# First round's indices loaded as four columns by two small transfers, its rows gathered by them, and the first query product ahead of the counts

## The chip, the cores and the metric

The kernel runs on one core of one Trainium2 chip. The metric is the device time of one execution in microseconds. Before the change three runs gave 676.91, 676.98 and 677.72, so the median is 676.98 us. The profiled execution took 677.21 us.

## What is computed

10,000 nodes with 512 features each (`x`) and 5,000 edges, sorted by destination (`src`, `dst`). One attention layer over the graph, then a small feed-forward layer and three normalisations:

```python
q = (h @ Wq).reshape(n, H, DK)          # H = 8 heads
k = (h @ Wk).reshape(n, H, DK)
v = (h @ Wv).reshape(n, H, DK)
e = jnp.einsum('ehd,ehd->eh', k[src], q[dst]) / sqrt(DK)
m = segment_max(e, dst);  ex = exp(e - m[dst]);  z = segment_sum(ex, dst)
a = segment_sum((ex / z[dst])[:, :, None] * v[src], dst)
x1 = layernorm(h + a @ Wo)
f = relu(x1 @ W1 + b1) @ W2 + b2
out = layernorm(h + layernorm(x1 + f))
```

Products are done once per edge, on gathered rows `x[dst]` and `x[src]`, and not once per node.

## The kernel before, in words

The 5,000 edges are worked through in 10 rounds of 500. A round gathers the 500 destination rows and 500 source rows (four indirect transfers of 125 rows each, `GXD` and `GXS`), turns them on TensorE (`TXD0` to `TXD3`, `TXS0` to `TXS3`, line 1025), splits each turned block into a high part (ScalarE, L521) and a low part (VectorE, L761), and multiplies: `Q0` to `Q3`, `K0` to `K3`, `V0` to `V3`, `O0` to `O3`. Each of these steps is 12 matmuls at L965: four blocks k of the contraction by three combinations (high by high, high by low, low by high). The scores, a running softmax in order of the edges and the feed-forward part for 1,000 rows of output per round (the slots `N0`, `N1`, `E0`, `E1`) follow.

Each engine has its order of steps written out: `PLAN` gives every step a due time, and `sequence` sorts by it. Steps with `!` are done once, ahead of or in round 0. In every engine the queue is strictly in that order; engines wait on each other by semaphores.

What happens once, at the start:

- SyncE loads the indices as 40 rows of 125 (`dst`, `src`, and `dst` shifted by one, L341 to L346), then Wq, Wk, small columns, W1 and the row of destinations (L348 to L357). It waits for the destination rows of round 0 (`xd_loaded`) before it issues Wv and W2 (L359, L361), and for the source rows (`xs_loaded`) before the rest, Wo last (L364 to L368).
- GpSimd sets constants (L378 to L409; among them `iota_b`, L398, 128 by 1024). Then come the gathers of round 0 (L412), which wait for the tables `dst_idx` and `src_idx`.
- VectorE casts the raw indices to floats (`CAST`, L657 and L660), TensorE turns them (`TURN`, L974 and L977), and VectorE writes the tables (`TABS`, L677 to L684). So an index passes a transfer, a cast, a transpose and a cast before a row is gathered by it.
- The rest of VectorE's chain (`FLAG`, `FILLI`, `DIG`) and TensorE's `OFFS` and `TURNF` prepare a list of the nodes that are no destination. It is made by counting: `CNT0` to `CNT4` on VectorE build one-hot tiles (L648, L643), two of each in turn, and `COUNT0` to `COUNT4` on TensorE multiply them (8 matmuls each, L1001). `CNT2` can only start when `COUNT0` is done, as it writes over the first buffer.
- `HQ` on ScalarE (L499) and `LQ` on VectorE (L636) split Wq into its high and low part.
- `FILLERS` puts matmuls whose result is not read (L1118) behind some steps: 8 behind `TURNF`, 2 behind each of `COUNT0`, `COUNT1`, `COUNT2`, 4 behind `TXD1`, 3 behind `TXD3`.

Order of the first steps before the change:

```
TensorE: TURN OFFS TURNF COUNT0 COUNT1 TXD0 TXD1 TXD2 TXD3 COUNT2 Q0 Q1 TXS0 TXS1 COUNT3 COUNT4 TXS2 Q2 ...
VectorE: CAST FLAG TABS FILLI DIG CNT0 CNT1 LQ TXD0 TXD1 CNT2 TXD2 TXD3 CNT3 CNT4 TXS0 TXS1 LK ...
ScalarE: HQ TXD0 TXD1 TXD2 TXD3 Q0 HK Q1 TXS0 TXS1 TXS2 HV TXS3 HO Q2 Q3 ...
```

Turned blocks go in turn to two banks (`pT`), so `TXD2` waits until the low part of block 0 has been taken, and `TXD3` for that of block 1. Products go in turn to three banks (`pP`). A product waits before its first matmul for all four low parts of its weights and of its rows.

Of the kernel before, what the change touches and what calls it, by code (L numbers as in the profile page):

```python
# [8 lines left out]
I32 = mybir.dt.int32  # L9
U32 = mybir.dt.uint32  # L10
# [12 lines left out]
SLOT_PERIOD = {"N0": 7687, "N1": 7689}  # L23
PLAN = {
    "pe": """
!TURN -276034; !FOLD -51782; !OFFS -237181; !TURNF -205187; !COUNT0 -202748; !COUNT1 -198663; !COUNT2 -146723;
!COUNT3 -94502; !COUNT4 -90190; !ROFF -71911; !BITS -8816; TXD0 -189819 -22912 125030 125323 125345;
TXS0 -102406 26305 131951 131437 131817; Q0 -138628 34546 131782 132194 129672; K0 -59911 65956 133983 133320 137209;
V0 27356 105501 136738 136738 170605; O0 89451 141151 143013 157654 247834; TXD1 -186065 -14365 126120 126712 125690;
TXS1 -100425 38188 132022 131705 131969; Q1 -106115 57936 132236 132221 132162; K1 -40813 69908 134313 133555 140512;  # L30
V1 33080 113889 136894 136880 181017; O1 106767 141614 143149 165755 248144; TXD2 -166405 -7868 129028 130799 126518;
# [43 lines left out]
E1.sq3 148558 148885 149937 229129 359991; <E1.z 149166 150501 150260 232611 340778  # L75
""",
    "dve": """
!CAST -263381; !FLAG -243336; !TABS -242836; !FILLI -241863; !FW -55094; !B1 -55229; !LQ -172721; !LK -85485;
!LV -54432; !LO 76605; !CNT0 -198287; !CNT1 -179760; !CNT2 -159099; !CNT3 -97504; !CNT4 -91086; !RANK -79616;
!DIG -211902; !LIST -79575; TXD0 -162172 -29587 125840 127315 124482; TXS0 -89151 40059 130890 130776 132032;  # L80
K0 -51732 66249 133633 132533 134452; W0 18249 122663 136307 136222 169476; N0 35421 125323 136834 136488 170118;
G0 49521 129368 137409 137177 185919; L0 44048 128784 137153 137940 187035; H0 89910 140875 142983 151481 211814;
TXD1 -161904 -24476 126177 127482 124895; TXS1 -88968 56437 131385 130810 132286;
K1 -49832 70573 134038 133868 136053; W1 29856 124303 136862 136864 179193; N1 42403 127213 136981 137078 182926;
G1 68839 133170 137965 140178 189672; L1 64124 130892 138184 139311 192048; H1 97516 140880 143008 152925 213212;
TXD2 -144446 7080 128832 130128 126147; TXS2 -67230 58549 131944 130850 132506; K2 -33982 77307 134316 133913 138039;
W2 61679 130905 137933 139380 191352; N2 70023 134152 138251 141899 191579; G2 76092 136480 140628 154187 213723;
L2 72234 139296 139912 145223 200118; H2 101683 143459 143493 165349 227378; TXD3 -114588 26350 129097 130197 126490;
TXS3 -57609 63218 132044 131711 132622; K3 -31718 80817 134898 134139 143486; W3 68959 138928 138383 140291 192894;
N3 81190 139073 139358 144215 193343; G3 111076 141990 141868 162698 225022; L3 84326 139475 140817 145509 203217;  # L90
H3 120939 144076 143627 166956 228551; mask -45989 55213 129213 134970 144639; A1 -39956 75393 134721 134045 136739;
# [69 lines left out]
def graph_attention(nc, x, src, dst, Wq, Wk, Wv, Wo, g1, be1, g2, be2, W1, b1, W2, b2, out):  # L161
    N, D = x.shape
    E = src.shape[0]
    DFF = W1.shape[1]
    P = 128
    KC = D // P
    HD = P // HEADS
    DK = D // HEADS
    R = 125
    EG = KC * R  # L170
# [6 lines left out]
    with ctx:  # L177
        def sb(name, shape, dt=F32):
            return ctx.enter_context(nc.sbuf_tensor(name, shape, dt))
# [23 lines left out]
        edge_idx = sb("edge_idx", [P, CT], I32)  # L203
        node_idx = sb("node_idx", [P, CT], I32)
        is_last = sb("is_last", [R, CT])

        xs = sb("xs", [P, 4, D])
        xd = sb("xd", [P, 4, D])
# [11 lines left out]
        weight = sb("weight", [P, EG])  # L220
# [50 lines left out]
        column_b = hots[:, 2 * (P + NL) * T8:2 * (P + NL) * T8 + NL]  # L271
        row_b, column_no, repeat_total = (att[:, 0, 100 + CT * n:140 + CT * n].bitcast(BF16)[:, 0:CT] for n in range(3))

        names = """dst_loaded idx_loaded wq_loaded wk_loaded wv_loaded wo_loaded w1_loaded b2_loaded w2_loaded all_loaded row_loaded
        zero_set ident_set ident_done head_set head_done below_set below_done iota_done init_done
        idx_cast idx_turned repeat_set repeat_summed offs_ready offs_done offs_kept fill_set fill_turned tables_done fill_kept
        split_hi split_lo w1_done b1_folded b1_done bias_loaded bits_set tables_clear
# [35 lines left out]
        def pP_of(i, step):  # L313
            return pP[place[i, step] % 3]
# [23 lines left out]
        @block.sync  # L338
        def _(sp):
            on = Waits(sp.wait_ge, s)  # L340
            sp.dma_start(idx_raw[0:CT, 1, :], dst.rearrange("(t e) -> t e", e=R)).then_inc(s["dst_loaded"], 16)  # L341
            sp.dma_start(idx_raw[0:CT, 0, :], src.rearrange("(t e) -> t e", e=R)).then_inc(s["idx_loaded"], 16)
            on.wait_ge("zero_set", 1)
            sp.dma_start(idx_raw[0:CT - 1, 2, :], dst[1:1 + (CT - 1) * R].rearrange("(t e) -> t e", e=R))\
                .then_inc(s["idx_loaded"], 16)
            sp.dma_start(idx_raw[CT - 1:CT, 2, 0:R - 1], dst[1 + (CT - 1) * R:E].rearrange("(t e) -> t e", t=1))\  # L346
                .then_inc(s["idx_loaded"], 16)
            sp.dma_start(stage["q"], Wq.rearrange("(k p) n -> p k n", p=P)).then_inc(s["wq_loaded"], 16)  # L348
            sp.dma_start(stage["k"], Wk.rearrange("(k p) n -> p k n", p=P)).then_inc(s["wk_loaded"], 16)
            with nc.allow_non_contiguous_dma("short columns, once"):  # L350
                sp.dma_start(g1_col[:, :], g1.rearrange("(k p) -> p k", p=P)).then_inc(s["w1_loaded"], 16)
                sp.dma_start(be1_col[:, :], be1.rearrange("(k p) -> p k", p=P)).then_inc(s["w1_loaded"], 16)
                for h in range(2):
                    sp.dma_start(b1_col[DFF * h:DFF * h + DFF, :], b1.rearrange("(f a) -> f a", a=1)).then_inc(s["w1_loaded"], 16)
            sp.dma_start(w1_raw, W1.rearrange("(k p) f -> p k f", p=P)).then_inc(s["w1_loaded"], 16)
            on.wait_ge("zero_set", 2)
            sp.dma_start(dst_row[:, 1:EG + 1], to_all(dst, EG)).then_inc(s["row_loaded"], 16)  # L357
            on.wait_ge("xd_loaded", 64)
            sp.dma_start(stage["v"], Wv.rearrange("(k p) n -> p k n", p=P)).then_inc(s["wv_loaded"], 16)  # L359
            for h in range(2):  # L360
                sp.dma_start(w2[DFF * h:DFF * h + DFF, :], W2).then_inc(s["w2_loaded"], 16)  # L361
            on.wait_ge("xs_loaded", 64)
            for tile, vec in ((g1_all, g1), (g2_all, g2)):
                sp.dma_start(tile[:, :], to_all(vec, D)).then_inc(s["all_loaded"], 16)  # L364
            sp.dma_start(bias_all[:, :], to_all(b2, D)).then_inc(s["b2_loaded"], 16)
            wo_rows = Wo.rearrange("(h m d) n -> h d m n", h=HEADS, m=KC)
            for h in range(HEADS):
                sp.dma_start(stage["o"][HD * h:HD * h + HD, :, :], wo_rows[h]).then_inc(s["wo_loaded"], 16)  # L368
            for i in range(1, ROUNDS):
                on.wait_ge("mask_eq", i)  # L370
                sp.dma_start(dst_row[:, :], bass.AP(tensor=dst.tensor, offset=dst.offset + (EG * i - 1), ap=[[0, P], [1, EG + 1]]))\
                    .then_inc(s["row_loaded"], 16)

        @block.gpsimd
        def _(pool):
            on = Waits(pool.wait_ge, s)
# [20 lines left out]
                               pattern=[[HD, HEADS], [0, HD]], channel_multiplier=-1).then_inc(s["head_done"], 1)  # L397
            pool.iota(iota_b, pattern=[[1, P], [0, T8]], base=0, channel_multiplier=0,  # L398
                      allow_small_or_imprecise_dtypes=True).then_inc(s["iota_done"], 1)
            pool.iota(column_b, pattern=[[1, NL]], base=0, channel_multiplier=0,  # L400
                      allow_small_or_imprecise_dtypes=True).then_inc(s["iota_done"], 1)
            pool.memset(ones_f, 1.0).then_inc(s["ones_set_f"], 1)
# [5 lines left out]
            pool.memset(eps_col[:, :], EPS).then_inc(s["init_done"], 1)  # L408
            pool.memset(carry[:, :], 0.0).then_inc(s["init_done"], 1)  # L409

            def gather(rows, table, column, name):
                pool.indirect_dma_start(rows, None, x, bass.IndirectOffsetOnAxis(ap=table[:, column:column + 1].bitcast(U32), axis=0),  # L412
                                        bounds_check=N - 1, oob_is_err=False).then_inc(s[name], 16)

            def scatter(rows, table, column, name):
                pool.indirect_dma_start(out, bass.IndirectOffsetOnAxis(ap=table[:, column:column + 1].bitcast(U32), axis=0), rows, None,  # L416
                                        bounds_check=N - 1, oob_is_err=False).then_inc(s[name], 16)

            for i, step in sequence("pool"):
                if step == "GXD":  # L420
                    on.wait_ge("tables_done", 1)
                    on.wait_ge("xd_turned", 4 * i)
                    for t in range(4):
# [514 lines left out]
        def _(pe):  # L938
# [20 lines left out]
                    j, old = products[n]  # L959
                    on.wait_ge({"Q": "q_saved", "K": "qk_part", "V": "weighted", "O": "hx_done"}[old[0]], 4 * j + int(old[1]) + 1)  # L960

            def split_product(acc, left, right):
                for k in range(KC):
                    for a, b in ((0, 0), (0, 1), (1, 0)):
                        ins = pe.matmul(acc, left(a, k), right(b, k), start=(k == 0 and a == b), stop=(k == KC - 1 and a == 1))  # L965
                return ins

            for i, step in pe_steps:
# [64 lines left out]
                elif "." not in step and step[0] in "QKV":  # L1033
                    m = int(step[1])
                    weight, xT, ready, number, filled = {"Q": (wq, xTd, "xd_lo", 1, "q_filled"), "K": (wk, xTs, "xs_lo", 2, "k_filled"),
                                                         "V": (wv, xTs, "xs_lo", 3, "v_filled")}[step[0]]
                    on.wait_ge("split_lo", number * KC)
                    on.wait_ge(ready, 4 * i + 4)
                    product_free(i, step)
                    split_product(pP_of(i, step)[:, 0:EG], lambda a, k: weight[a][:, k, P * m:P * m + P], lambda b, k: xT[b][:, k, :])\  # L1040
                        .then_inc(s[filled], 1)
                elif "." not in step and step[0] == "O":
                    t = int(step[1])
                    on.wait_ge("split_lo", 4 * KC)
# [98 lines left out]
```

## Time and profile before

| what | value |
|---|---|
| median of 3 runs | 676.98 us |
| profiled execution | 677.21 us, its span 675.5 us |
| TensorE (PE) busy | 642.1 us, 95% |
| VectorE (DVE) busy | 577.7 us, 86% |
| ScalarE (ACT) busy | 528.3 us, 78% |
| GpSimd (POOL) busy | 402.4 us, 60% |

"Busy" is the time in which an engine had an instruction in work. All times below are counted from the start of the span. A timeline row gives the start, the duration, engine, line, operation, output and inputs, how many instructions were merged, and in brackets the idle time ahead of it with what ended that.

### The profile page before, as it was taken

How to read it: one execution, taken by the hardware profiler on the slowest of the kernel's cores; microseconds unless marked ns; L12 is line 12 of the kernel's file. 1: busy time of each engine (PE TensorE's matmuls, PEld its weight loads, DVE VectorE, ACT ScalarE, POOL GpSimd, SP SyncE). 2: the span in 40 equal slices, each digit the busy share in tenths (PEclk: the TensorE clock that was granted, in tenths of full speed). 3: DMA queues.
4: the chain of work that ended last, by engine and by line, in shares of the span. 5: the costliest groups of instructions: out<-in, count | busy, mean ns of one | idle time of the engine just before them, and what ended most of it. 6: DMA issues, size and time to landing. Idle time of an engine off the chain costs nothing. (4 is left out here: it accounts for less than half of the span.)

```text
span 675.5 us, 10865 instructions
## 1 busy us (share of the span) xinstructions
PE 642.1 (95%) x3520; PEld 483.8 (72%) x3520; DVE 577.7 (86%) x1391; ACT 528.3 (78%) x1140; POOL 402.4 (60%) x363
## 2 busy tenths in 40 slices
PE   5999999999999999999999999999999999999980
PEld 2778877777777777777777777777778777775640
DVE  7668769979898898898979898988889899899885
ACT  2525259987888988898798789879888999699784
POOL 7268343767575865766676664864456834836435
PEclk9999999999999999999999999999999999999996
DMA  7844154744643644583475347456353743634563
GB/s 229 219 106 132 41 122 105 182 126 137 154 124 122 161 132 133 161 183 81 133 183 131 102 153 156 108 152 155 93 150 123 194 92 89 185 74 114 132 125 122
DMA packets 37748, 91.44 MB, mean 135 GB/s; under 512 B 8347, under 2 KB 9643, under 8 KB 37691
## 3 DMA queue, kind: packets, MB, share of 16 engines
q0 software_dynamic: 31536, 82.74, 48.0%
q1 hardware_dynamic: 6154, 8.01, 4.2%
q8 instruction: 28, 0.46, 0.3%
q14 instruction: 30, 0.24, 0.1%
HBM read 71.20 MB, written 20.99 MB: 136 GB/s over the span
## 5 line engine op out<-in xcount | busy, mean ns | idle before, releaser
L560 ACT ACTIVATE squares<-rows,nmean 125x512 bf16<-125x512 f32 x200 | 142.2, 713 | 41.8 <-DVE nmean L904 19.4
L416 POOL DMA_INDIRECT out_dram<-rows,node_idx x40 | 46.5, 1163 | 59.4 <-ACT rows L620 39.1
L412 POOL DMA_INDIRECT x_rows<-in_x_dram,node_idx x40 | 48.1, 1203 | 56.8 <-DVE rows L919 47.3
L475 POOL DMA_DIRECT2D x_rows<-in_L_gnn_ln_b_dram x40 | 52.9, 1372 | 31.2 <-DVE rows L823 21.7
L900 DVE SCALAR_TENSOR_TENSOR rows<-pF,rows 125x512 f32<-125x512 f32 x78 | 50.6, 686 | 22.8 <-PE pF L1105 22.1
L965 PE MATMUL pP<-wo_hi,aT_hi 128*125 128x512 f32 x160 | 65.9, 412 | 0.3 <-DVE aT_lo L850 0.3
L965 PE MATMUL pP<-xTs_hi,wv_hi 128*128 128x500 f32 x160 | 65.7, 411 | 0.0
L965 PE MATMUL pP<-xTd_hi,wq_hi 128*128 128x500 f32 x160 | 65.4, 409 | 0.1
L965 PE MATMUL pP<-xTs_hi,wk_hi 128*128 128x500 f32 x160 | 63.5, 397 | 0.0
L965 PE MATMUL pP<-wo_lo,aT_hi 128*125 128x512 f32 x160 | 63.1, 394 | 0.0
L965 PE MATMUL pP<-wo_hi,aT_lo 128*125 128x512 f32 x160 | 63.0, 394 | 0.0
L965 PE MATMUL pP<-xTs_hi,wk_lo 128*128 128x500 f32 x160 | 62.4, 390 | 0.0
L965 PE MATMUL pP<-xTd_lo,wq_hi 128*128 128x500 f32 x160 | 62.4, 390 | 0.0
L965 PE MATMUL pP<-xTs_hi,wv_lo 128*128 128x500 f32 x160 | 62.3, 390 | 0.0
L965 PE MATMUL pP<-xTd_hi,wq_lo 128*128 128x500 f32 x160 | 62.2, 389 | 0.0
L965 PE MATMUL pP<-xTs_lo,wv_hi 128*128 128x500 f32 x160 | 62.1, 388 | 0.0
L965 PE MATMUL pP<-xTs_lo,wk_hi 128*128 128x500 f32 x160 | 62.1, 388 | 0.0
L416 POOL DMA_INDIRECT out_dram<-rows,edge_idx x40 | 43.6, 1091 | 29.3 <-ACT rows L620 19.8
L412 POOL DMA_INDIRECT x_rows<-in_x_dram,edge_idx x40 | 44.5, 1113 | 27.2 <-issue 11.3
L620 ACT ACTIVATE rows<-rows,shift,rs 125x512 f32<-125x512 f32 x76 | 57.4, 805 | 1.4 <-DVE shift L935 1.4
L919 DVE SCALAR_TENSOR_TENSOR rows<-rows,rs,x_rows 125x512 f32<-125x512 f32 x80 | 57.1, 751 | 1.2 <-DMA x_rows<-in_L_gnn_ln_b_dram 0.9
L909 DVE SCALAR_TENSOR_TENSOR rows<-rows,nmean,g_all 125x512 f32<-125x512 f32 x80 | 57.6, 761 | 0.2
(197 smaller groups left out, 1761.8 us busy)
## 6 DMA issues: line engine op xcount, KB each, us to landing
x_rows<-in_L_gnn_ln_b_dram POOLq DMA_DIRECT2D x40, 512.0 KB, 6.6
dst_row<-in_dst_dram SPq DMA_DIRECT2D x9, 250.5 KB, 3.6
q<-in_L_gnn_Wq_dram SPq DMA_DIRECT2D x1, 1024.0 KB, 5.6
rows<-in_L_gnn_Wk_dram SPq DMA_DIRECT2D x1, 1024.0 KB, 7.9
rows<-in_L_gnn_Wv_dram SPq DMA_DIRECT2D x1, 1024.0 KB, 7.5
x_rows<-in_L_gnn_Wo_dram SPq DMA_DIRECT2D x8, 128.0 KB, 5.6
xd<-in_x_dram,dst_idx POOLq DMA_INDIRECT x40, 4.3
xs<-in_x_dram,src_idx POOLq DMA_INDIRECT x40, 3.8
```

What stands on the lines that cost most here:

```text
L412: pool.indirect_dma_start(rows, None, x, bass.IndirectOffsetOnAxis(ap=table[:, column:column + 1].bitcast(U32), axis=0), bounds_check=N - ...
L416: pool.indirect_dma_start(out, bass.IndirectOffsetOnAxis(ap=table[:, column:column + 1].bitcast(U32), axis=0), rows, None, bounds_check=N ...
L475: pool.dma_start(xr_wide[n], bass.AP(tensor=be2.tensor, offset=be2.offset, ap=[[0, P], [0, 2], [1, D]]), accum_op=ALU.add).then_inc(s[f"be ...
L560: ins = act.activation(squares[:, t, :], w[n][:, t, :], ACT.Square, bias=nmean[c][n][:, t:t + 1], accum_out=sq[c][n][:, t:t + 1])
L620: ins = act.activation(w[n][:, t, :], w[n][:, t, :], ACT.Identity, scale=rs[3][n][:, t:t + 1], bias=shift[n][:, t:t + 1])
L900: dve.scalar_tensor_tensor(w[n][:, t, :], f_banks(i, slot)[t][0:R, :], 1.0, w[n][:, t, :], ALU.mult, ALU.add, accum_out=sums[2][n][:, t:t ...
L909: ins = dve.scalar_tensor_tensor(w[n][:, t, :], w[n][:, t, :], nmean[2][n][:, t:t + 1], g2_all[0:R, :], ALU.add, ALU.mult)
L919: ins = dve.scalar_tensor_tensor(w[n][:, t, :], w[n][:, t, :], rs[2][n][:, t:t + 1], xr[n][:, t, :], ALU.mult, ALU.add, accum_out=sums[3][ ...
L965: ins = pe.matmul(acc, left(a, k), right(b, k), start=(k == 0 and a == b), stop=(k == KC - 1 and a == 1))
```

## The change

The first four rows of 125 indices are loaded a second time, ahead of everything else, as columns: tile `first_dst` and tile `first_src`, 125 partitions by 4. Round 0's gathers take their row numbers from these, with no cast or transpose. The gathers of `xd` move in GpSimd's queue from behind its constants to behind `iota_b`; those of `xs` stay in their place in the queue. Wv and W2 wait for the source rows and no longer for the destination rows. The count steps 0 and 1 go behind `Q0` on TensorE; on VectorE `LQ` and the four `TXD` go ahead of all five `CNT`. A product waits for its low parts block by block. The new order is:

```
TensorE: TURN OFFS TURNF TXD0 TXD1 TXD2 TXD3 Q0 COUNT0 COUNT1 COUNT2 Q1 TXS0 TXS1 COUNT3 COUNT4 ... (as before)
VectorE: CAST FLAG TABS FILLI DIG LQ TXD0 TXD1 TXD2 TXD3 CNT0 CNT1 CNT2 CNT3 CNT4 TXS0 TXS1 LK ... (as before)
ScalarE, GpSimd: the order of steps is as before
```

The fillers keep their steps.

```diff
+        first_idx = [sb(f"first_{n}", [R, KC], I32) for n in ("dst", "src")]
@@ sync
+            with nc.allow_non_contiguous_dma("one round's indices, once"):
+                for tile, indices, name in zip(first_idx, (dst, src), ("first_dst", "first_src")):
+                    sp.dma_start(tile[:, :], indices[0:EG].rearrange("(t e) -> e t", e=R)).then_inc(s[name], 16)
             sp.dma_start(idx_raw[0:CT, 1, :], dst.rearrange("(t e) -> t e", e=R)).then_inc(s["dst_loaded"], 16)
...
-            on.wait_ge("xd_loaded", 64)
+            on.wait_ge("xs_loaded", 64)
             sp.dma_start(stage["v"], Wv.rearrange("(k p) n -> p k n", p=P)).then_inc(s["wv_loaded"], 16)
...
-            on.wait_ge("xs_loaded", 64)
@@ gpsimd
+            def first_gather(rows, which, name):
+                on.wait_ge(("first_dst", "first_src")[which], 16)
+                for t in range(4):
+                    gather(rows[0:R, t, :], first_idx[which], t, name)
+
+            first_gather(xd, 0, "xd_loaded")
             pool.iota(column_b, pattern=[[1, NL]], base=0, channel_multiplier=0,
                       allow_small_or_imprecise_dtypes=True).then_inc(s["iota_done"], 1)
...
             for i, step in sequence("pool"):
-                if step == "GXD":
+                if step == "GXD" and i == 0:
+                    continue
+                elif step == "GXS" and i == 0:
+                    first_gather(xs, 1, "xs_loaded")
+                elif step == "GXD":
@@ tensor
-            def split_product(acc, left, right):
+            def split_product(acc, left, right, weights=None, columns=None):
                 for k in range(KC):
+                    if columns:
+                        on.wait_ge("split_lo", weights + k + 1)
+                        on.wait_ge(columns[0], columns[1] + k + 1)
...
-                    on.wait_ge("split_lo", number * KC)
-                    on.wait_ge(ready, 4 * i + 4)
                     product_free(i, step)
...
+                                  (number - 1) * KC, (ready, 4 * i)).then_inc(s[filled], 1)
```

## Rows read from the trace of the kernel before

**Rows 1.** Windows by stage: length, busy per engine, then PEclk, DMA share, GB/s
```profile
0.00:21.20 21.20, 12.92 (x67) 6.78 (x68) 15.98 (x47) 5.71 (x9) 13.96 (x29) 1.00 0.79 246
...
245.00:310.00 65.00, 65.00 (x360) 50.02 (x359) 58.35 (x143) 55.94 (x125) 44.05 (x37) 1.00 0.55 137
...
640.00:675.50 35.50, 14.45 (x99) 7.82 (x98) 25.68 (x77) 22.84 (x57) 14.88 (x13) 0.82 0.45 117
```

**Rows 2.** Waits of PE over the whole span: sum, times, longest
```profile
PE pT L1025 <- DMA xd<-in_x_dram,dst_idx: 1.4, 1, 1.4
```

**Rows 3.** Timeline of PE, the first 36 us
```profile
8.42 3.59 PE L1118 MATMUL pP<-below 128*128 128x512 bf16 x8
...
14.06 0.60 PE L1118 MATMUL pP<-below 128*128 128x512 bf16 x2
16.03 1.07 PE L1025 MATMUL pT<-ident,xd 125*128 125x125 f32 x8 [1.37 <-DMA xd<-in_x_dram,dst_idx]
...
19.13 0.81 PE L1118 MATMUL pP<-below 128*128 128x512 bf16 x3
19.99 0.69 PE L1001 MATMUL pS<-x_rows 125*128 125x80 bf16 x8
...
21.20 0.47 PE L965 MATMUL pP<-xTd_hi,wq_hi 128*128 128x500 f32 x1
...
24.02 0.39 PE L965 MATMUL pP<-xTd_hi,wq_hi 128*128 128x500 f32 x1
...
35.84 0.39 PE L965 MATMUL pP<-xTs_hi,wk_hi 128*128 128x500 f32 x1
```

**Rows 4.** Timeline of POOL, the first 12 us
```profile
2.94 1.95 POOL L398 IOTA nT<- 128x1024 bf16 x1
4.84 0.29 POOL L400 IOTA x_rows<- 128x80 bf16 x1
...
7.69 1.21 POOL L412 DMA_INDIRECT xd<-in_x_dram,dst_idx  x1 [1.80 <-DVE is_last L682]
...
11.83 1.13 POOL L412 DMA_INDIRECT xd<-in_x_dram,dst_idx  x1 [0.30 <-issue]
```

**Rows 5.** Timeline of DVE, the first 21 us
```profile
2.53 0.22 DVE L657 CAST ex<-ex 40x125 f32<-40x125 int32 x1 [1.34 <-DMA ex<-in_dst_dram]
3.26 1.77 DVE L660 CAST ex<-ex 40x125 f32<-40x125 int32 x2 [0.52 <-DMA ex<-in_dst_dram]
...
10.66 0.69 DVE L648 TENSOR_TENSOR x_rows<-nT,att 125x1024 bf16<-125x1024 bf16 x1
...
13.34 2.49 DVE L636 TENSOR_TENSOR wq_lo<-q,wq_hi 128x512 fp32r<-128x512 f32 x4
...
19.84 1.26 DVE L761 TENSOR_TENSOR xTd_lo<-pT,xTd_hi 128x500 fp32r<-128x500 f32 x2
```

**Rows 6.** Round 0's gathers by tile (xd): issue to landing
```profile
DMA to landing us min/median/max: 4.1/4.4/4.7
```

**Rows 7.** Round 0's gathers by tile (xs): issue to landing
```profile
DMA to landing us min/median/max: 3.9/6.4/7.6
```

**Rows 8.** DMA queues, window 10 to 11 us: packets, MB, share of 16 engines
```profile
DMA packets 993, 0.28 MB, mean 285 GB/s; under 512 B 949, under 2 KB 952, under 8 KB 993
...
q1 hardware_dynamic: 952, 0.13, 80.9%
q0 software_dynamic: 41, 0.16, 48.8%
```

**Rows 9.** Timeline of SP's queue (SPq), the first 17 us
```profile
0.82 0.40 SPq L341 DMA_DIRECT2D ex<-in_dst_dram  x1
...
2.29 0.41 SPq L348 DMA_DIRECT2D q<-in_L_gnn_Wq_dram  x1
...
16.00 0.37 SPq L359 DMA_DIRECT2D rows<-in_L_gnn_Wv_dram  x1
```

**Rows 10.** Timeline of ACT, 29 to 33 us
```profile
29.95 2.18 ACT L499 ACTIVATE wv_hi<-rows 128x512 fp32r<-128x512 f32 x4
```

More of the change, by code:

```diff
@@ L25 @@
     "pe": """
-!TURN -276034; !FOLD -51782; !OFFS -237181; !TURNF -205187; !COUNT0 -202748; !COUNT1 -198663; !COUNT2 -146723;
+!TURN -276034; !FOLD -51782; !OFFS -237181; !TURNF -205187; !COUNT0 -150500; !COUNT1 -150000; !COUNT2 -146723;
 !COUNT3 -94502; !COUNT4 -90190; !ROFF -71911; !BITS -8816; TXD0 -189819 -22912 125030 125323 125345;
-TXS0 -102406 26305 131951 131437 131817; Q0 -138628 34546 131782 132194 129672; K0 -59911 65956 133983 133320 137209;
+TXS0 -102406 26305 131951 131437 131817; Q0 -151000 34546 131782 132194 129672; K0 -59911 65956 133983 133320 137209;
 V0 27356 105501 136738 136738 170605; O0 89451 141151 143013 157654 247834; TXD1 -186065 -14365 126120 126712 125690;
@@ L77 @@
     "dve": """
-!CAST -263381; !FLAG -243336; !TABS -242836; !FILLI -241863; !FW -55094; !B1 -55229; !LQ -172721; !LK -85485;
-!LV -54432; !LO 76605; !CNT0 -198287; !CNT1 -179760; !CNT2 -159099; !CNT3 -97504; !CNT4 -91086; !RANK -79616;
-!DIG -211902; !LIST -79575; TXD0 -162172 -29587 125840 127315 124482; TXS0 -89151 40059 130890 130776 132032;
+!CAST -263381; !FLAG -243336; !TABS -242836; !FILLI -241863; !FW -55094; !B1 -55229; !LQ -205000; !LK -85485;
+!LV -54432; !LO 76605; !CNT0 -185000; !CNT1 -179760; !CNT2 -159099; !CNT3 -97504; !CNT4 -91086; !RANK -79616;
+!DIG -211902; !LIST -79575; TXD0 -190000 -29587 125840 127315 124482; TXS0 -89151 40059 130890 130776 132032;
 K0 -51732 66249 133633 132533 134452; W0 18249 122663 136307 136222 169476; N0 35421 125323 136834 136488 170118;
 G0 49521 129368 137409 137177 185919; L0 44048 128784 137153 137940 187035; H0 89910 140875 142983 151481 211814;
-TXD1 -161904 -24476 126177 127482 124895; TXS1 -88968 56437 131385 130810 132286;
+TXD1 -189500 -24476 126177 127482 124895; TXS1 -88968 56437 131385 130810 132286;
 K1 -49832 70573 134038 133868 136053; W1 29856 124303 136862 136864 179193; N1 42403 127213 136981 137078 182926;
 G1 68839 133170 137965 140178 189672; L1 64124 130892 138184 139311 192048; H1 97516 140880 143008 152925 213212;
-TXD2 -144446 7080 128832 130128 126147; TXS2 -67230 58549 131944 130850 132506; K2 -33982 77307 134316 133913 138039;
+TXD2 -189000 7080 128832 130128 126147; TXS2 -67230 58549 131944 130850 132506; K2 -33982 77307 134316 133913 138039;
 W2 61679 130905 137933 139380 191352; N2 70023 134152 138251 141899 191579; G2 76092 136480 140628 154187 213723;
-L2 72234 139296 139912 145223 200118; H2 101683 143459 143493 165349 227378; TXD3 -114588 26350 129097 130197 126490;
+L2 72234 139296 139912 145223 200118; H2 101683 143459 143493 165349 227378; TXD3 -188500 26350 129097 130197 126490;
 TXS3 -57609 63218 132044 131711 132622; K3 -31718 80817 134898 134139 143486; W3 68959 138928 138383 140291 192894;
@@ L272, in graph_attention @@
         row_b, column_no, repeat_total = (att[:, 0, 100 + CT * n:140 + CT * n].bitcast(BF16)[:, 0:CT] for n in range(3))
-        names = """dst_loaded idx_loaded wq_loaded wk_loaded wv_loaded wo_loaded w1_loaded b2_loaded w2_loaded all_loaded row_loaded
+        names = """first_dst first_src dst_loaded idx_loaded wq_loaded wk_loaded wv_loaded wo_loaded w1_loaded b2_loaded w2_loaded all_loaded row_loaded
         zero_set ident_set ident_done head_set head_done below_set below_done iota_done init_done
@@ L399, in _, with gather, scatter @@
                       allow_small_or_imprecise_dtypes=True).then_inc(s["iota_done"], 1)
+            def gather(rows, table, column, name):
+                pool.indirect_dma_start(rows, None, x, bass.IndirectOffsetOnAxis(ap=table[:, column:column + 1].bitcast(U32), axis=0),
+                                        bounds_check=N - 1, oob_is_err=False).then_inc(s[name], 16)
+            def scatter(rows, table, column, name):
+                pool.indirect_dma_start(out, bass.IndirectOffsetOnAxis(ap=table[:, column:column + 1].bitcast(U32), axis=0), rows, None,
+                                        bounds_check=N - 1, oob_is_err=False).then_inc(s[name], 16)
+            def first_gather(rows, which, name):
[3 more added lines that the diff above has]
+            first_gather(xd, 0, "xd_loaded")
             pool.iota(column_b, pattern=[[1, NL]], base=0, channel_multiplier=0,
@@ L409, in _ @@
             pool.memset(carry[:, :], 0.0).then_inc(s["init_done"], 1)
[L411 to L417, printed above, removed]
-            for i, step in sequence("pool"):
-                if step == "GXD":
+            for i, step in sequence("pool"):
+                if step == "GXD" and i == 0:
[3 more added lines that the diff above has]
+                elif step == "GXD":
                     on.wait_ge("tables_done", 1)
@@ L1036, in _ @@
                                                          "V": (wv, xTs, "xs_lo", 3, "v_filled")}[step[0]]
-                    on.wait_ge("split_lo", number * KC)
-                    on.wait_ge(ready, 4 * i + 4)
                     product_free(i, step)
-                    split_product(pP_of(i, step)[:, 0:EG], lambda a, k: weight[a][:, k, P * m:P * m + P], lambda b, k: xT[b][:, k, :])\
-                        .then_inc(s[filled], 1)
+                    split_product(pP_of(i, step)[:, 0:EG], lambda a, k: weight[a][:, k, P * m:P * m + P], lambda b, k: xT[b][:, k, :],
+                                  (number - 1) * KC, (ready, 4 * i)).then_inc(s[filled], 1)
                 elif "." not in step and step[0] == "O":
```

## The prediction

> **What bounds the kernel now.** I read the page first (TensorE 95% busy), then the windows by stage. In the middle of the kernel TensorE has no idle time at all: 65.00 of 65.00 us [rows 1]. Idle TensorE stands only in the first 21.2 us (12.92 busy) and in the last 35 [rows 1]. From the start of `Q0` on, TensorE works through one queue, so whatever moves the first products moves the end by the same amount, provided the matmuls behind them are the same ones, and they are. The tail (14.45 busy of 35.50) hangs on the last rows and moves along with them. So the change is worth what it does to one moment, the start of `Q1`, because from `Q1` on the order on TensorE is unchanged. Before, `Q1` starts at 24.02 [rows 3].
>
> The waits of TensorE name what counts ahead of it: 1.4 us for the gathered destination rows [rows 2], which ends at 16.03 [rows 3]. I call that moment T. From T to `Q1` it took 24.02 - 16.03 = 7.99 us.
>
> **When T comes now.** The gathers of `xd` no longer wait for the tables. They wait for `first_dst`, and stand behind `iota_b`, which ends at 2.94 + 1.95 = 4.89 [rows 4]. The small transfer is the first on SyncE: the first transfer before was issued at 0.82 [rows 9] and used at 2.53 [rows 5], 1.7 us later. This one has 500 packets of 4 bytes. Its price is bounded by the window from 10 to 11 us, where 952 packets, nearly all small, took 80.9% of 16 engines: 12.9 / 952 = 13.6 ns each [rows 8], so 500 are 0.43 us over 16 engines. Even at 1.5 us more it is there before 4.89. So I let the first gather start at 5.2, 0.3 after the iota (the gap between gathers) [rows 4]; if the gap that the first one had before is its own preparation, 5.9. From first to fourth it was 11.83 - 7.69 = 4.14 us [rows 4], so the fourth is issued at 9.34. It then needs 3.9 us at the least and 7.6 at the most [rows 6, 7]. The 7.6 is from `xs` behind Wv; the four of `xd` had 4.1 to 4.7, and I take 4.7, as now all four run beside Wq and Wk. T = 9.34 + 4.7 = 14.0, or 2.0 us earlier. Ends: 13.2 (3.9), and 15.5 (start 5.9 and some 0.8 more for sharing).
>
> A row bears on that sharing: between 10 and 11 us the gathers' queue moved 0.16 MB and SyncE's queue 0.13 [rows 8]. At 0.16 MB per us the 1.0 MB of four gathers takes 6.4 us. The Trainium skill (DMA: Bandwidth & Descriptors, Queues, rings and completion order) says that each DMA engine takes the queues in turn, packet by packet, so a queue does not get ahead by being first; by it the earlier gathers run slower than before, and T would be nearer 14.6 than 14.0.
>
> **What T waits for besides.** TensorE must have done the 8 fillers. They start after VectorE's chain of casts. Two more transfers ahead on SyncE, at 0.4 each to 0.5 [rows 9], shift the raw indices by about 0.9 us, to which 1,000 packets add up to 0.85. It would look as if the chain went back by 1 to 1.8 us, but the trace says otherwise: the two casts at L660 start at 3.26 and last until 5.03, where the same cast at L657 takes 0.22 [rows 5]. They end together with GpSimd's iota at 4.89 [rows 4]. So the casts have been held up by the iota; indices that come up to 1.6 us later still give casts that end at 5.0 to 5.2. I take 0.1 us for the chain. It costs up to 0.8 if the transfers take the upper bound. The fillers then end at 8.42 + 3.59 + 0.1 = 12.1 [rows 3], before T; this is also the floor under T. `LQ` follows the chain: VectorE is free for it at 10.66 + 0.1 [rows 5], Wq comes about 1 us later, and `LQ` ends at about 13.5, before the first low part (T + 1.3). Cover is about 1.8 us.
>
> **From T to `Q1` now.** Transposes and the 7 fillers are as before: the last three start at 19.13 [rows 3], T + 3.10, and end 0.68 later, T + 3.8. `Q0` follows. The low parts of blocks 2 and 3 come sooner than before, as `CNT2` no longer stands between them; the last is done at about T + 4.6 (19.84 + 1.26 - 0.5 [rows 5] less 16.03), and only the matmuls from T + 5.9 need it: no wait. `Q0` lasts 24.02 - 21.20 = 2.82 [rows 3], to T + 6.6. Then `COUNT0`, `COUNT1`, `COUNT2`, each with 2 fillers: 21.20 - 19.99 = 1.21 each [rows 3], 3.63 in all, if their one-hot tiles are ready. A `CNT` takes (13.34 - 10.66) / 2 = 1.34 [rows 5]: ready at T + 6.0, 7.3 and, since `CNT2` also waits for `COUNT0` (T + 7.2), 8.7. TensorE wants them at 6.6, 7.8 and 9.0. So `Q1` starts at T + 10.2: 7.99 before plus two counts (2.4) less the 0.2 wait ahead of `COUNT2`. This is where the gain goes: before, two counts with their fillers stood in time in which TensorE had nothing else to do; now they stand behind T.
>
> **The rest.** Block by block waits: 3 more per round for Q and K each, 60 in all, and 9 once. `K0` of round 0 had three waits ahead of it and its first matmul started at 35.84 at the ordinary pace, with no extra duration (0.39) [rows 3], so waits already met cost nothing; if each cost the 0.08 us that a first matmul sometimes has on top (0.47 at 21.20), 5 us. I take 0. They gain nothing either, as TensorE has no idle time to lose. Source rows: gathers from about 11.7 to 16.7, landed by 20 to 23.5; wanted at T + 13. Wv is now issued then and not at 16.00 [rows 9]; at 7.5 us it lands by 27.5 to 31, and its split starts at 29.95 [rows 10] and ends 18 us ahead of `V0`. No cost; if that cover went, ScalarE's `TXS3` behind it would be late by up to 1 us, which TensorE has not yet to wait for. `CNT3`, `CNT4` end about T + 11.4, before VectorE's 4 us of idle time are used up.
>
> **Sum.** 14.0 + 10.2 - 24.02 = +0.2 us. The profiled execution took 677.21, 0.23 above the median of the runs, so the forecast for a median is 677.21 + 0.2 - 0.23 = 677.2 us. About 0.2% (1.35 us) is what I take measurement to tell from no change.
>
> **The rivals.**
> 1. *The clock is still low at T (slower).* The fillers at 8.42 took 0.449 us each, those at 14.06 0.30 or less [rows 3], though the profile's granted clock reads 1.00 for this whole stretch [rows 1]. So TensorE ran at 1.2 GHz until about 13.5 and at 2.4 after, and before the change it had worked from 8.42 on with hardly a break until that rise. Now it works to 12.1 and pauses for 2 us. If the rise comes only after T, transposes, fillers and `Q0` run at half pace for a while: all of it to the end of `Q0` would cost 7 x 0.22 (fillers) + 12 x 0.2 (`Q0`) + 0 to 2 (transposes; no slow row) = 3.9 to 5.9 us; a rise 3 us after T about 1.2 to 1.5. Against it: 3.6 us of fillers may do. Decides: whether the first fillers behind `TXD1` are 0.22 or 0.45 apart. Time 678.5 to 683, most likely 678.7. The Trainium skill (TensorE: Matmul & The Clock Gate, Part 1) says that sustained work releases the low clock and that the moment varies between runs; the trace agrees on the first, and by it this rival would come in some runs and not in others.
> 2. *The rows come as early as the fillers allow (faster).* T = 12.1 gives 12.1 + 10.2 - 24.02 = -1.7: 675.3. Speaks for it: SyncE's traffic is lighter behind 12 us. Against: it needs 2.8 us from issue to landing, and the least shown is 3.9 [rows 7], which gives -0.6, 676.4.
> 3. *The small transfers hold up what is behind them.* Indices past 4.89 by 1 to 1.5 us, fillers to 13.5, `LQ` to 15: T + 1.3 is missed by about 0.7. +0.7 to +1.3: 677.9 to 678.5.
> 4. *The change does less than it says*: the first gather is not started before 6 or 7 us. T = 15.5: +1.7, 678.7.
>
> **Chances.** Forecast with its own range (676.3 to 677.9) 0.52; rival 1 0.22; rival 2 0.12; rival 3 0.08; rival 4 0.06. Faster by over 0.2%: most of rival 2 and a little for a gain I don't see, 0.15. Slower by over 0.2%: most of 1 and 4, part of 3, 0.25. Within: 0.60. The range 675.8 to 679.0 takes in the nearer part of the rivals.
>
> **What would show it.** First gather at 5.2 and last landing near 14.0; casts that end with the iota at about 5.0; fillers done at 12.1, then about 2 us of idle TensorE; `Q0` at about 17.8; `Q1` at 24.2, then no wait. Wrong if `Q1` starts more than 1.3 us from 24.0, or if time moves while `Q1` does not.

## The result and the profile after

The changed kernel takes 684.73 us (median of 4 runs, 684.3 to 685.67) against 676.98 before: ratio 1.011, interval 1.0097 to 1.0123. It is 7.75 us slower by the medians (7.4 by the ratio). I had forecast 677.2 with a range that ended at 679.0. The profiled execution took 685.67 us, span 684.0.

Timeline of PE in the kernel after (start, duration, ...; answers to rows 3):

```profile
8.37 3.49 PE L1132 MATMUL pP<-below 128*128 128x512 bf16 x8
19.79 1.93 PE L1041 MATMUL pT<-ident,xd 125*128 125x125 f32 x8 [7.93 <-DMA xd<-in_x_dram,first_dst]
21.51 1.91 PE L1132 MATMUL pP<-below 128*128 128x512 bf16 x4
23.22 1.87 PE L1041 MATMUL pT<-ident,xd 125*128 125x125 f32 x8
24.88 1.01 PE L1132 MATMUL pP<-below 128*128 128x512 bf16 x3
25.55 0.58 PE L981 MATMUL pP<-xTd_hi,wq_hi 128*128 128x500 f32 x1
...
31.45 0.58 PE L981 MATMUL pP<-xTd_hi,wq_hi 128*128 128x500 f32 x1
```

`Q1` starts at 31.45 and not at 24.02 [rows 3]: 7.4 us later, and this is nearly the whole loss. It has two parts. The rows come at 19.79 and not at 16.03: +3.8. And from there to `Q1` it takes 11.66 and not 7.99: +3.7. From `Q1` on the two traces run nearly in step. This execution loses one more us in a wait of 0.62 us for source rows at 133 us and what follows it; in `e2_wide_load` below, with the same gathers, that wait is absent and the time nearly the same, so it is not needed for the result.

Timeline of POOL after (answers to rows 4):

```profile
2.94 1.95 POOL L401 IOTA nT<- 128x1024 bf16 x1
5.11 1.45 POOL L404 DMA_INDIRECT xd<-in_x_dram,first_dst  x1 [0.21 <-issue]
...
10.03 1.28 POOL L404 DMA_INDIRECT xd<-in_x_dram,first_dst  x1 [0.30 <-issue]
```

The first gather starts at 5.11 (forecast 5.2) and the fourth at 10.03 (forecast 9.34): each takes 1.27 to 1.45 us of GpSimd's time and not 1.00 to 1.21. The failure is behind them. The time from a gather's issue to its landing (the moment when its rows are in SBUF), round 0's `xd` by tile (answers to rows 6), kernel after:

```profile
DMA to landing us min/median/max: 8.6/9.1/9.7
```

Twice the 4.1 to 4.7 of before, and more than the 7.6 that I had as the worst. What the clock did meanwhile, windows of the kernel after (length, busy per engine, PEclk, DMA share, GB/s; answers to rows 1):

```profile
14.00:19.00 5.00, 0.00 (x0) 0.00 (x0) 0.00 (x0) 0.00 (x0) 4.00 (x4) 0.60 1.12 220
19.00:22.00 3.00, 2.21 (x10) 1.88 (x11) 0.46 (x1) 0.83 (x2) 0.00 (x0) 0.50 0.94 203
22.00:26.00 4.00, 4.00 (x17) 2.75 (x16) 1.83 (x4) 1.52 (x3) 0.00 (x0) 0.59 0.32 77
26.00:32.00 6.00, 5.82 (x44) 4.32 (x43) 5.91 (x10) 2.66 (x5) 0.00 (x0) 1.00 1.02 321
```

TensorE stood idle from 11.9 to 19.79. The granted clock reads 0.60 in 14 to 19 us and 0.50 in 19 to 22, so the first transposes and fillers ran at 1.2 GHz, half of 2.4 (four fillers in 1.91 us, eight transposes in 1.93 against 1.07 [rows 3]).

The timeline of DVE after (answers to rows 5) bears out what I read from the casts:

```profile
3.99 0.98 DVE L670 CAST ex<-ex 40x125 f32<-40x125 int32 x1 [2.80 <-DMA ex<-in_dst_dram]
4.62 0.54 DVE L673 CAST ex<-ex 40x125 f32<-40x125 int32 x2
```

The raw indices came 1.5 us later (cast at 3.99 and not 2.53), the last of them still ended at 5.16, just behind the iota (4.89), where before it was 5.03, and the fillers started at 8.37, even 0.05 sooner than before. That the iota is what holds them is read from these ends; no run moves it.

### The profile page after: what moved, and what is told of

It reads as the page before. It is cut to its first block and busy times, and to the rows that moved or that the text cites. A ratio compares the mean times of both kernels' runs of the same rounds, so it can differ in the third digit from the quotient of the medians.

```text
span 684.0 us, 10867 instructions
## 1 busy us (share of the span) xinstructions
PE 643.7 (94%) x3520; PEld 485.4 (71%) x3520; DVE 577.5 (84%) x1391; ACT 528.3 (77%) x1140; POOL 402.8 (59%) x363
## 3 DMA queue, kind: packets, MB, share of 16 engines
q0 software_dynamic: 32688, 82.75, 48.2%
```

## The experiments

All times are medians beside runs of the kernel before in the same set (677.56, 677.36 and 677.11 us for the three sets). The ratio to it is given with its 95% interval. Runs of different sets are compared by these ratios.

### Set 1: which transfer is slow

Both new kinds of transfer, the index columns and the gathers by them, were 125 partitions wide; the gathers of before were 128. `e1_wide_both`:

```diff
-        first_idx = [sb(f"first_{n}", [R, KC], I32) for n in ("dst", "src")]
+        first_idx = [sb(f"first_{n}", [P, KC], I32) for n in ("dst", "src")]
-                    sp.dma_start(tile[:, :], indices[0:EG].rearrange("(t e) -> e t", e=R))
+                    sp.dma_start(tile[:, :], bass.AP(tensor=indices.tensor, offset=indices.offset, ap=[[1, P], [R, KC]]))
-                    gather(rows[0:R, t, :], first_idx[which], t, name)
+                    gather(rows[:, t, :], first_idx[which], t, name)
```

> The changed kernel with 128 partitions in place of 125 in the two index transfers and in the eight gathers of round 0 (the last three indices are simply the next three of the list; their rows are gathered and never read). Theory N (a gather of 125 rows is laid out worse than one of 128 and lands 8.6 to 9.7 us after issue for that reason): landing back to 4 to 5 us, destination rows there at 14 to 15, Q1 at 24 to 26, time 677 to 679. Rival B (the gathers are slow because they are issued early and share the DMA engines with Wq and Wk): landing stays near 9, rows at 19 to 20, time about 684. Rival S (the 4-byte index transfers clog the queues): with 128 partitions they are no less packets, so it would expect little: 683 to 684.

Measured: 679.47 us, ratio 1.0036 (1.0022 to 1.005); rows at 14.92, `Q1` at 26.14. Time and `Q1` lie just above what theory N gave. Its profile has no landing of `xd`. The fourth gather was issued at 9.21 and the rows were there 5.7 us later; `e5_more_fillers`, with the same transfers, shows all four:

```profile
DMA to landing us min/median/max: 5.7/6.3/7.0
```

So they land 2 to 4 us sooner than in the changed kernel, but not in the 4 to 5 us that theory N expected.

`e2_wide_load`: the first two changes of that diff; the gathers keep `rows[0:R, t, :]`.

> The changed kernel with only the two index transfers widened to 128 partitions; the gathers stay at 125 rows. Theory N: rows of xd still land about 9 us after issue, time 683.5 to 685. Rival S with the 125-partition form as the cause (transfers of 125 partitions take long and hold up all behind them): much of the loss comes back, 678 to 681. Rival B: 684.

Measured: 685.11 us, ratio 1.0115 (1.0098 to 1.0132). Landing 7.9/9.1/10.2, rows at 20.30.

`e3_wide_gather`: the third change only. The index tiles get 128 partitions and are set to `SKIP` (out of bounds) beforehand, and the index transfers, still of 125, wait for that.

> The changed kernel with only the gathers widened to 128 rows (the index tiles are set to an out-of-bounds number beforehand, and SyncE waits for that, some 0.3 us); the index transfers stay at 125 partitions. Theory N: 677 to 679.5, at most 1.5 us above the kernel with both widened. Rival S: 682 to 684. Rival B: 684.

Measured: 679.37 us, ratio 1.0029 (1.0018 to 1.0039). Rows at 15.25.

`e4_before_narrow`, in the kernel before:

```diff
-                        gather(xd[:, t, :], dst_idx, 4 * i + t, "xd_loaded")
+                        gather(xd[0:R, t, :] if i == 0 else xd[:, t, :], dst_idx[0:R, :] if i == 0 else dst_idx, 4 * i + t, "xd_loaded")
```

(and the same for `xs`).

> The kernel before the change with only round 0's eight gathers narrowed to 125 rows. Theory N: landing of xd 8 to 9 us instead of 4.4, the rows come 3 to 5 us later and so does the end: 680 to 682. Rival B and rival S: no change, 677.

Measured: 681.52 us, ratio 1.006 (1.0044 to 1.0077). Rows at 18.75, 2.7 us later than before: the fourth gather was issued at 12.76 and not at 11.83, and its rows were there 6.0 us later and not 4.2. The time is as theory N gave it, the rows are a little under its 3 to 5 us, and the landing is far under its 8 to 9. Here too the first transposes were slow behind a gap of 4.19 us (1.88 us), so that `Q0` started 3.6 us late.

The four agree on the cause. In either kernel gathers of 125 rows bring the rows later than gathers of 128; the width of the index transfers makes no difference that these runs can tell. Theory N holds; rival S falls, and so does rival B as an account of its own. But the size depends on the surroundings: the same narrowing costs 2.7 us in the kernel before and 4.5 to 5.4 in the changed one, where the gathers are issued earlier, beside Wq and Wk. Profile of `e1_wide_both`, `xd` by tile and timeline of PE:

```profile
L404 POOL DMA_INDIRECT xd<-in_x_dram,first_dst x4: 998/1005/1212, 5.1 to 9.2; - x4
```

```profile
14.92 1.93 PE L1041 MATMUL pT<-ident,xd 125*128 125x125 f32 x8 [2.97 <-DMA xd<-in_x_dram,first_dst]
16.64 1.91 PE L1132 MATMUL pP<-below 128*128 128x512 bf16 x4
...
26.14 0.57 PE L981 MATMUL pP<-xTd_hi,wq_hi 128*128 128x500 f32 x1
```

Even so 2 us are lost: the first transposes (1.93) and fillers (1.91) still run at the low clock. Here this is read from their durations; the granted clock of this profile reads 1.00 for 15 to 18 us, as it did for the slow fillers of the kernel before [rows 1, 3].

### Set 2: the order and the clock

`e5_more_fillers`, from `e1_wide_both`:

```diff
-    (0, "TURNF"): 8,
+    (0, "TURNF"): 16,
```

> The kernel with both widened (rows at 14.9, Q1 at 26.1), with 16 in place of 8 fillers behind TURNF, so that TensorE works on until about 14.5. Theory C (TensorE fell to, or stayed at, 1.2 GHz because it had 3 us of nothing to do ahead of the first transposes; that costs 1.0 to 1.4 us up to Q1): the first eight transposes take 1.07 and not 1.93, Q1 at 24.9 to 25.2, time 1.0 to 1.3 below the kernel with both widened. Rival (the clock is not to blame, the transposes are slow as they follow on a DMA): no change, or slower by what the fillers run over.

Measured: 678.13 us, ratio 1.001 (0.9996 to 1.0023), 0.26% (1.7 us) below `e1_wide_both` by the ratios. Timeline of PE in its profile:

```profile
8.35 5.94 PE L1132 MATMUL pP<-below 128*128 128x512 bf16 x16
14.98 1.07 PE L1041 MATMUL pT<-ident,xd 125*128 125x125 f32 x8 [0.69 <-DMA xd<-in_x_dram,first_dst]
15.89 1.03 PE L1132 MATMUL pP<-below 128*128 128x512 bf16 x4
...
24.45 0.57 PE L981 MATMUL pP<-xTd_hi,wq_hi 128*128 128x500 f32 x1
```

The rows come at the same time (14.98), the transposes take 1.07, and T to `Q1` is 9.47 and not 11.22. The clock it was, and it costs 1.7 us by the traces, somewhat more than the 1.0 to 1.4 expected. My 10.2 for T to `Q1` was 0.7 too high for the high clock.

`e6_old_order`: `e1_wide_both` with the due times of before (COUNT0, COUNT1 and CNT0, CNT1 ahead of the transposes).

> The kernel with both widened, with the order of before on TensorE and VectorE (COUNT0 and COUNT1 ahead of the transposes, CNT0, CNT1 ahead of LQ). My account of the order (two counts with their fillers, 2.4 us, stand in a gap if they are ahead of T and on the path if behind it; besides they keep TensorE at its high clock): Q1 at 14.9 + 8.0 plus up to 0.6 for an LQ that ends near 16.8, so 22.9 to 23.6, time 2.5 to 3.2 below the kernel with both widened, 0.4 to 1.1 below the kernel before. Rival (the new order is the part that helps, by taking the counts off the way to Q0): time above that of the kernel with both widened.

Measured: 676.89 us, ratio 0.9993 (0.9979 to 1.0008); rows taken up at 15.40, `Q1` at 23.44. That is 2.9 us below `e1_wide_both` by the ratios (`Q1`: 2.7 sooner), within its expectation; from the kernel before it is not told apart.

`e7_order_only`: the changed kernel with the SyncE and GpSimd programs of before, so new order and block waits alone.

> The kernel before with only the new order and the waits block by block; indices, gathers and transfers as before, so rows at 16.0. My account: the fillers end at 12.0, 4 us of idle TensorE follow, the transposes start at the low clock, Q1 at 16.0 + 11.2 = 27.2 to 27.7, time 680 to 681. Rival (order helps or is neutral): 676.5 to 677.5.

Measured: 680.7 us, ratio 1.0046 (1.0033 to 1.0059). Timeline of PE:

```profile
8.42 3.59 PE L1119 MATMUL pP<-below 128*128 128x512 bf16 x8
16.40 1.93 PE L1028 MATMUL pT<-ident,xd 125*128 125x125 f32 x8 [4.39 <-DMA xd<-in_x_dram,dst_idx]
...
28.27 0.58 PE L968 MATMUL pP<-xTd_hi,wq_hi 128*128 128x500 f32 x1
```

So the new order is a loss of 3.1 us by itself, as expected, though `Q1` in this profile comes at 28.27 and not by 27.7: T to `Q1` is 11.87, and the rows came at 16.40, as the third and fourth gather took 1.50 us each here. It takes the two counts out of a gap, and by making the gap longer (4.39 us) it lets the transposes, fillers and part of the rest start at 1.2 GHz.

`e8_wk_later`, from `e6_old_order`:

```diff
-            sp.dma_start(stage["k"], Wk.rearrange("(k p) n -> p k n", p=P)).then_inc(s["wk_loaded"], 16)
...
             sp.dma_start(dst_row[:, 1:EG + 1], to_all(dst, EG)).then_inc(s["row_loaded"], 16)
+            on.wait_ge("xd_loaded", 64)
+            sp.dma_start(stage["k"], Wk.rearrange("(k p) n -> p k n", p=P)).then_inc(s["wk_loaded"], 16)
             on.wait_ge("xs_loaded", 64)
```

> The kernel with both widened and the old order, with Wk issued only when the destination rows are there. In all kernels so far the first packet of the gathers moves at 9.8 to 10.2 us, whether the first gather is issued at 5.1 or at 7.7, about when Wk's packets run out. Theory Q (the gathers' packets wait behind Wq and Wk): with Wk gone the first packet moves at about 7 to 8.5, rows at 12.8 to 13.8, time up to 1 us below the kernel with the old order. Rival (a gather needs that time for itself, its descriptors are written slowly): first packet still at 9.8, rows at 14.9, no change of time.

Measured: 679.94 us (677.66 to 683.34), ratio 1.0038 (1.0016 to 1.0059): slower, which neither theory said. The DMA queues of 8 to 9.5 us, first in `e6_old_order`, then in `e8_wk_later`:

```profile
q1 hardware_dynamic: 293, 0.58, 100.3%
```

```profile
q1 hardware_dynamic: 1163, 0.07, 53.3%
q0 software_dynamic: 78, 0.26, 44.9%
```

With Wk in the way no packet of the gathers moved in that time (no row for q0), without it 78 did. So theory Q is right about the packets, and Wk's load is part of what delays the rows: the fourth gather's rows landed at 14.3. But TensorE was busy with `COUNT1` and its fillers until 15.08 and took them up only then. Wk does not hold them back to its end, though. In `e1_wide_both` the two queues share from 10 to 12 us, while Wk still loads (it was issued at 3.8 and took 9.7 us):

```profile
q1 hardware_dynamic: 234, 0.39, 52.6%
q0 software_dynamic: 118, 0.41, 50.3%
```

`Q1` came at 22.72, 1.3 us before its time in the kernel before. The loss is 17 us further on. Timelines of `e8_wk_later`, ACT, then PE:

```profile
37.55 2.19 ACT L516 ACTIVATE wo_hi<-x_rows 128x512 fp32r<-128x512 f32 x4 [5.62 <-DMA x_rows<-in_L_gnn_Wo_dram]
```

```profile
40.26 0.79 PE L982 MATMUL pP<-xTs_hi,wk_hi 128*128 128x500 f32 x1 [2.03 <-ACT q L555]
40.85 0.62 PE L982 MATMUL pP<-xTs_lo,wk_hi 128*128 128x500 f32 x1
```

Wk, now later, ran beside the source rows, these landed at 21.6, and all that SyncE issues behind that wait, Wo last, came later. ScalarE waited 5.6 us for Wo with `Q2`'s copy behind it in its queue, TensorE waited 2.0 us for the bank, and went on at the low clock (0.62 per matmul and not 0.39; granted clock 0.50 in 40 to 43 us). A wait of 0.6 us for source rows at 128 us adds nearly one more.

### Set 3: the version that follows, and how rows are dealt out

`e9_wo_sooner`, from `e8_wk_later`: W2, g1 and g2 issued behind Wo and not ahead of it.

> The kernel with both widened, old order and Wk late, with W2 and the two rows g1, g2 issued behind Wo. In the run with Wk late Q1 was already at 22.7, 1.3 us ahead of before, but ScalarE waited 5.6 us for Wo at its split, saved Q2 late, and TensorE stood still for 2.0 us ahead of K1 and came back at the low clock; the end was 3 us late. Account W (that wait alone took the gain): with Wo issued some 2 us sooner the wait ahead of K1 goes or shrinks below 0.5, K1 at 38.2 to 38.8, time 1.0 to 1.5 below the kernel before, 675.5 to 676.5. Rival (Wk late costs elsewhere too, by the source rows): still at or above 677.

Measured: 676.89 us against 677.11, ratio 0.9988 (0.9979 to 0.9998). `Q1` at 22.55, the wait ahead of `K1` 0.3. It is the only version whose interval lies below 1: 0.8 us faster than the kernel before by the ratio (0.2 by the medians), less than the 1.0 to 1.5 expected. Account W holds for the wait. What Wk late is worth by itself is not shown: the intervals of `e6_old_order` and `e9_wo_sooner` overlap, and the 0.9 us by which `Q1` is sooner in this profile than in that of `e6_old_order` go with the clock, which was already high behind `COUNT0` here and not there. First `e6_old_order`, then `e9_wo_sooner`:

```profile
13.17 1.05 PE L1132 MATMUL pP<-below 128*128 128x512 bf16 x2
...
15.40 1.46 PE L1041 MATMUL pT<-ident,xd 125*128 125x125 f32 x8
```

```profile
13.15 0.60 PE L1133 MATMUL pP<-below 128*128 128x512 bf16 x2
...
14.93 1.02 PE L1042 MATMUL pT<-ident,xd 125*128 125x125 f32 x8
```

`e10_fewer_fillers`: `e9_wo_sooner` with `(0, "TXD3"): 0` and `(0, "COUNT2"): 0`.

> The same with Wo sooner, without the 3 fillers behind TXD3 and the 2 behind COUNT2. They are between T and Q1 and last 0.68 + 0.45 us. If they cover a wait (COUNT2's one-hot tiles, the last low part), Q1 comes 0 to 0.5 sooner; if they are pure work, 1.1 sooner. The high clock should hold, as no gap is over 1 us. Time 0 to 1.1 below the kernel with Wo sooner; if the clock falls, 1 us above it.

Measured: 676.6 us, ratio 0.9995 (0.998 to 1.0009). Not told apart from `e9_wo_sooner`. Its one profile had the low clock at the first transposes (1.87 us for eight, where `e9_wo_sooner` had 1.02, with the same work ahead of them), so the two profiles can't be compared for the fillers. Inconclusive.

`e11_rows_127` and `e12_rows_126`, from `e1_wide_both`:

```diff
-                    gather(rows[:, t, :], first_idx[which], t, name)
+                    gather(rows[0:127, t, :], first_idx[which][0:127, :], t, name)     # 0:126 in e12
```

> The kernel with both widened, with gathers of 127 rows. In the changed kernel the eight gathers of 125 rows left 480 packets of two rows, 40 of one row and 1056 of 8 bytes: per gather 5 engines with 25 rows each (12 pairs and one) and 11 engines with 12 packets of 8 bytes that carry nothing. Theory D (rows are dealt out evenly, over the largest number of engines up to 16 that divides them): 127 is prime, so one engine moves all 127, 63 pairs at 0.16 us, about 10 us per gather; landing 12 us or more, rows at 22 to 27, time 686 to 691. Theory N without D (anything but 128 is laid out in the bad way): as with 125 rows, landing about 9, rows at 19.8, time 684 to 685.

Measured (one run): 704.87 us, rows at 28.95. Both are far beyond theory D's 691 and 27. `Q1` came at 39.52, 13.4 us later than in `e1_wide_both`, and another 12 us are lost behind it: TensorE waited 1.8 us for the source rows, whose gathers are of 127 rows too, and 6.9 us ahead of `K1` for ScalarE's copy of `q`, the wait of `e8_wk_later` once more.

> The kernel with both widened, with gathers of 126 rows. Theory D: 14 engines with 9 rows each, so 4 pairs and one per engine: landing 4 to 5, rows at 14.9 to 15.5, time as with 128, 678.5 to 680. Theory N without D: landing about 9, time 684 to 685.

Measured (one run): 680.57 us, rows at 16.47. Landing was 7.0 to 8.0 us and the rows came 1 us later than theory D's latest, so it had the times for 126 rows too low as well, though theory N without D was further off (landing 9, 684 to 685 us). What decides for theory D are the packets.

Packets of the gathers' queue over the whole kernel (packets, MB, share), in this order: after, `e1_wide_both`, `e11_rows_127`, `e12_rows_126`:

```profile
q0 software_dynamic: 32688, 82.75, 48.2%
```

```profile
q0 software_dynamic: 31536, 82.79, 48.1%
```

```profile
q0 software_dynamic: 39216, 82.83, 47.4%
```

```profile
q0 software_dynamic: 31664, 82.75, 49.1%
```

Theory D gives these numbers. With k engines for n rows a gather has n/k rows on each of k engines, in packets of two rows and one single if the number is odd; the other 16 - k engines get as many packets that carry nothing, and each of the 16 one for the semaphore. For 128 rows (k = 16): 64 + 16 = 80. For 125 (k = 5): 5 x 13 + 11 x 13 + 16 = 224, so 144 more for each of 8 gathers, 1152: 32688 - 31536 = 1152. For 127 (k = 1): 16 x 64 + 16 = 1040, 8 x 960 = 7680: 39216 - 31536 = 7680. For 126 (k = 14): 14 x 5 + 2 x 5 + 16 = 96, 8 x 16 = 128: 31664 - 31536 = 128. All three are exact. The 125 was known when the theory was made; 126 and 127 were not. The records do not name the engine of a packet, so k is inferred from these counts. The Trainium skill (DMA: Bandwidth & Descriptors, Why a DMA increments its semaphore by 16 and not by 1) has this rule: the number of DMA engines is the largest up to 16 that divides the slowest dimension of both sides, and 127 partitions get one. These runs agree, for indirect gathers too.

## Why the prediction was wrong

**T, the failed step.** "The four of `xd` had 4.1 to 4.7, and I take 4.7", with 3.9 to 7.6 as bounds: all of these rows are of gathers with 128 partitions. (The "four indirect transfers of 125 rows each" of my description were wrong for the same reason: `xd[:, t, :]` in the kernel before names 128, with an index out of bounds in the last three.) The changed gathers name `rows[0:R]`, 125, and so, by their packets, move by 5 DMA engines in place of 16. I read the diff for what waits for what and took the shape to be the same. T was forecast at 14.0 and was 19.79. Of the 5.8 us, 4.5 to 5.4 are the shape (19.79 - 15.25 with the gathers alone widened; 20.30 - 14.92 with the wide transfers in both). The rest, 0.9 (14.92 against 14.0), goes with the company of Wq and Wk: the fourth gather of 128 rows, issued at 9.21, needed 5.7 us and not 4.7. That I had bounded (15.5).

The Trainium skill (DMA: Bandwidth & Descriptors, Queues, rings and completion order) lets each DMA engine take the queues in turn, packet by packet; by it I had weighed a T nearer to 14.6. The trace agrees from 10 us on (0.41 MB for the gathers' queue and 0.39 for SyncE's in 2 us); that the gathers move nothing from 8 to 9.5 us, with the first issued at 5.1, it does not explain.

**T to `Q1`: mechanism right, one size missing.** Forecast 10.2, measured 11.66. `Q0` lasted from 25.55 to 28.47 (2.9, as forecast), and three counts with fillers to 31.45, 3.0 against 3.6. From T to `Q0` it took 5.76 against 3.8. That is rival 1, the low clock: at the high clock `e5_more_fillers` needed 3.57 for the same steps, so it cost 2.2 us in the changed kernel (and 1.7 in `e1_wide_both`) against the 1.2 to 1.5 that I gave for a rise 3 us after T. The 11.66 lies nearer to the forecast than the mechanism deserves, as the counts, forecast 0.6 too long, hid a part of it. I gave rival 1 a chance of 0.22; it was the case in the changed kernel and, with the narrow gathers cured, in `e1_wide_both` and `e3_wide_gather` too. So even with the gathers wide the change is 2 to 2.4 us slower, not 0.2. That is 678.9 to 679.4 on the scale of the first runs, about the end of my range.

**That the order costs what the transfers gain**: right in direction, not in size. By themselves, order +3.1 us (`e7_order_only`), transfers with wide gathers -0.5 (`e6_old_order`, an interval that takes in zero), both +2.4. I had +2.2 against -2.0.

**The casts under the iota**: right as far as the ends show it (casts end at 5.16, fillers start at 8.37), and so rival 3 did not come. **Block by block waits at nothing**: right to about 0.1 us over 10 rounds; `e1_wide_both` is 2.5 us behind the kernel before at 77 us and 2.4 at 599. The first matmul of a product behind fillers is 0.1 longer (0.58 against 0.47).

**Wv behind the source rows**: no cost in the changed kernel, as said. But the same wait set the end in `e8_wk_later`, by way of Wo and not of Wv; I had counted Wv's cover and not Wo's. In the kernel before ScalarE already waited for Wo until 36.7.

**Still open**: 25 rows per engine in place of 8 are 17 x 0.08 = 1.4 us more at the 0.16 us of a packet of two rows, an estimate from the packets. In the kernel before the fourth gather's landing became 1.8 us longer by the narrowing (6.0 against 4.2), not far from it. In the changed kernel it became 4.0 longer (9.7 against the 5.7 of `e1_wide_both`), and 0.8 came from the longer issue of the four (1.27 us each and not 1.00; fourth at 10.03 and not 9.21). What makes the difference between 1.8 and 4.0 was not separated; that Wq and Wk on the same engines do it is argued, not shown.

## What to carry to other kernels

Read a changed transfer for its shape first: gathers of 125 rows went over 5 DMA engines by their packets and brought the rows 2.7 to 5.4 us later than gathers of 128, and 127 rows, over one, made the kernel 28 us slower than before (one run); rounding up to 128, with three rows nobody reads, took that away. Work taken from a wait and put behind it is paid twice where TensorE then comes back at its low clock: once for the work, once for the clock. And when a transfer is moved behind another wait, follow all that stands behind it in the same queue up to the last one that somebody waits for.

## What the runs showed that I had not expected

- A gather's packets may not move for a long time while 2 MB of weights load by SyncE's queue: issued at 5.1, none from 8 to 9.5 us and one in 8 to 10 in the kernel after. From 10 us on they share with Wk.
- GpSimd's own time per gather goes with its packets and not with its rows: 1.00 us for 128 rows (80 packets), 1.07 for 126 (96), 1.27 for 125 (224) and 2.6 to 2.9 for 127 (1040); the first gather takes some 0.2 more.
- The clock differed between profiles of nearly the same program: with the same work ahead of them the first eight transposes took 1.02 us in `e9_wo_sooner` and 1.87 in `e10_fewer_fillers`. That is 0.8 us in the transposes alone, and it is as large as the gain of `e9_wo_sooner` itself.
